# A decoder layer on one core: an opening in another order, accumulators summed two or three steps later, four tiles of the last half added on POOL

## The reference

```
x = layernorm(x + self(x))                 # 32 heads of 16, attention over the heads of one token
x = layernorm(x + cross(x, ctx_4096))      # below
x = layernorm(x + ffn(x))                  # router 64, softmax, top 8, mix of expert biases

cross: kv = concat([ctx (1601), x (256)])           # 1857 keys a batch
       q = rms_norm(x @ Wq) * qw                     # 32 heads of 128
       k = rms_norm(kv @ Wk) * kw;  v = kv @ Wv      # 8 heads of 128, 4 query heads share one
       probs = softmax(q k^T / sqrt(128));  out = (probs v) @ Wo
```

## Time and profile before

| | |
|---|---|
| median of 3 runs | 2776.49 us (2775.12 to 2777.37) |
| profiled execution | 2775.53 us, span 2773.7 us |
| PE / PEld | 2697.6 (97%) / 2188.7 (79%) |
| DVE / ACT / POOL | 2129.3 (77%) / 2097.7 (76%) / 2326.0 (84%) |
| chain of waits | PE 78%, POOL 8%, issue 7%, DVE 5%, ACT 2%, DMA 1% |

### The profile page before, as it was taken

One profiled execution on the slowest core, in us unless ns is written; L12 is line 12 of the kernel. 1 busy time (PEld: TensorE's weight loads), 2 busy tenths in 40 slices (PEclk: granted clock), 3 DMA queues, 4 the chain that ended last, 5 costly groups with the idle time before them and its releaser, 6 DMA issues.

```text
span 2773.7 us, 47580 instructions
## 1 busy us (share of the span) xinstructions
PE 2697.6 (97%) x14620; PEld 2188.7 (79%) x14620; DVE 2129.3 (77%) x3497; ACT 2097.7 (76%) x4202; POOL 2326.0 (84%) x2300
## 2 busy tenths in 40 slices
PE   7899999999999999999999999999999999999996
PEld 5777778777787888888888888888888888888763
DVE  5578777887787777777777777777777878887787
ACT  3587787787777777777788788788887877777773
POOL 4299899898888888888888888889888888888883
PEclk9999999999999999999999999999999999999998
DMA  7656655655655555555556555445544534454321
GB/s 238 241 192 216 205 200 184 219 197 178 211 175 172 180 174 179 180 183 167 171 172 203 173 183 190 158 172 169 197 157 165 189 130 163 152 167 165 121 69 42
DMA packets 160794, 485.36 MB, mean 175 GB/s; under 512 B 18583, under 2 KB 29337, under 8 KB 160542
## 3 DMA queue, kind: packets, MB, share of 16 engines
q1 hardware_dynamic: 158952, 480.75, 51.1%
q10 hardware_dynamic: 1590, 1.58, 0.2%
HBM read 402.83 MB, written 79.43 MB: 174 GB/s over the span
## 4 chain that ended last, share of the span: by engine, by line
PE 78%; POOL 8%; issue 7%; DVE 5%; ACT 2%; DMA 1%; SPq 0%; POOLq 0%; DVEq 0%; ACTq 0%
PE K_ps L1003 9%; PE K_ps L1005 9%; PE K_ps L1004 8%; PE OT_ps L1033 7%; PE S_ps L1003 7%; PE S_ps L1005 6%; PE S_ps L1004 6%; PE OT_ps L1003 5%; POOL acc L938 5%; PE OT_ps L1004 4%; PE OT_ps L1005 4%; POOL P_lo L920 2%; PE F_ps L1003 2%; PE F_ps L1004 2%; PE F_ps L1005 2%
## 5 line engine op out<-in xcount | busy, mean ns | idle before, releaser
L938 POOL TENSOR_TENSOR acc<-acc,scores 128x512 f32<-128x512 f32 x813 | 1068.6, 1314 | 50.7 <-ACT scores L1375 23.3
L920 POOL TENSOR_TENSOR P_lo<-scores,P_hi 128x512 fp32r<-128x512 f32 x672 | 901.3, 1342 | 220.8 <-ACT scores L1375 220.1
L1723 DVE SCALAR_TENSOR_TENSOR running_max<-S_ps,rk,running_max 128x512 f32<-128x512 f32 (+1 forms) x896 | 667.9, 745 | 272.9 <-ACT scores L1361 270.5
L1707 DVE TENSOR_TENSOR scores<-scores,Mb_ps 128x512 f32<-128x512 f32 (+1 forms) x960 | 645.5, 672 | 138.8 <-PE Mb_ps L1159 138.8
L1361 ACT ACTIVATE scores<-S_ps,rk 128x512 f32<-128x512 f32 (+1 forms) x960 | 652.3, 679 | 122.2 <-PE S_ps L1005 107.8
L1374 ACT ACTIVATE P_hi<-scores 128x512 fp32r<-128x512 f32 x672 | 423.4, 630 | 298.3 <-DVE scores L1707 209.5
L1375 ACT ACTIVATE scores<-scores 128x512 f32<-128x512 f32 (+1 forms) x960 | 596.7, 622 | 13.5 <-DVE scores L1707 11.9
L1003 PE MATMUL S_ps<-QT_hi,KT_hi 128*128 128x512 f32 (+1 forms) x960 | 495.5, 516 | 15.6 <-DVE running_max L1723 13.8
L1003 PE MATMUL K_ps<-Wkv_hi,kvT 128*128 128x256 f32 (+1 forms) x1664 | 470.1, 283 | 2.4 <-DVE kvT L1773 2.4
L1005 PE MATMUL K_ps<-Wkv_hi,kvT 128*128 128x256 f32 (+1 forms) x1664 | 470.3, 283 | 0.0
L1004 PE MATMUL K_ps<-Wkv_lo,kvT 128*128 128x256 f32 (+1 forms) x1664 | 469.0, 282 | 0.0
(11 more groups left out here) (244 smaller groups left out, 4577.2 us busy)
## 6 DMA issues: line engine op xcount, KB each, us to landing
kvT<-kvT_scratch SPq DMA_DIRECT2D x403, 512.0 KB, 3.9
Wq_hi<-weight_halves_scratch SPq DMA_DIRECT2D x48, 512.0 KB, 6.1
Wq_lo<-weight_halves_scratch SPq DMA_DIRECT2D x48, 512.0 KB, 6.7
Wo_hi<-weight_halves_scratch SPq DMA_DIRECT2D x48, 512.0 KB, 4.6
Wo_lo<-weight_halves_scratch SPq DMA_DIRECT2D x48, 512.0 KB, 5.7
kvT_scratch<-built SPq DMA_DIRECT2D x45, 512.0 KB, 4.2
rinv_spread<-rinv_scratch SPq DMA_DIRECT2D x63, 256.0 KB, 5.1
Wkv_hi<-weight_halves_scratch SPq DMA_DIRECT2D x24, 512.0 KB, 5.4
```

Source lines behind the costliest of these rows:

```text
L920: e.tensor_tensor(P_lo[n % PB][0:r, :], prob(t)[0:r, :], f(P_hi[n % PB][0:r, :]), ALU.subtract)\
L938: e.tensor_tensor(a[0:r, :], a[0:r, :], prob(t)[0:r, :], ALU.add).then_inc(s_acc, 1)
L1707: e.tensor_tensor(d, d, Mb_ps[0:r, :], ALU.add).then_inc(s_d, 1)
L1723: e.scalar_tensor_tensor(a, src, k, a, ALU.mult, ALU.max).then_inc(s_top, 1)
```

## The change

Three parts. First, the opening: before the first score stand KV tiles 0 to 8 (9 before), context tiles up to 11 (13), and self projections 0 to 5 (all 8); projections 5, 6, 7 go to steps -3, 3, 7. Both query tiles are normalised in one step (`normed`), QT(0, 0) goes from step -1 to -4, a Q product waits for its own half of Wq_lo only, and the self-attention's sums stand in another order. Odd context tiles of the first batch use OT_n in place of row[0] as their staging buffer. Second, for v < 32, AT of the odd half goes from c = 10 to 12 and of the even half from c = 25 to 28, with all that hangs on it. Third, in the last half tiles 0, 1, 6, 7 leave SUMMED: POOL adds them (three instructions), and DVE sums acc once.

```diff
--- before.py
+++ after.py
@@ -71,9 +71,9 @@
     TOP = 8
     FULL = [[2, 3, 6, 7, 10, 11, 14], [4, 5, 10, 11, 14], [6, 7, 14], [6, 7, 14]]
     FULL = [FULL[v // KVH] for v in range(UNITS)]
-    SUMMED = [[] for p in range(HALVES - 2)] + [[2, 4, 6, 8, 10, 12], list(range(NJ))]
+    SUMMED = [[] for p in range(HALVES - 2)] + [[2, 4, 6, 8, 10, 12], [2, 3, 4, 5, 8, 9, 10, 11, 12, 13, 14]]
     ADDED = [NJ * p + j for p in range(HALVES) for j in range(1, NJ) if j not in SUMMED[p]]
-    LATE = [p for p in range(HALVES) if len(SUMMED[p]) == NJ]
+    LATE = [HALVES - 1]
     ADD_AT = {t: n for n, t in enumerate(ADDED)}
     HALF = [[j for j in range(NJ) if j not in FULL[v]] for v in range(UNITS)]
     HALF_TILES = [NJ * p + j for p in range(HALVES) for j in HALF[p // 2]]
@@ -101,31 +101,30 @@
 
     OPENING = {
         -20: [("X", 0, 2)],
-        -19: [("X", 0, 3)],
-        -18: [("X", 0, 4)],
-        -17: [("KV", 0, 0)],
+        -18: [("X", 0, 3)],
+        -17: [("X", 0, 4), ("KV", 0, 0)],
         -16: [("KV", 0, 1)],
         -15: [("X", 0, 5)],
         -14: [("KV", 0, 2)],
         -13: [("KV", 0, 3), ("X", 0, 6)],
-        -12: [("X", 0, 7)],
-        -11: [("KV", 0, 4), ("KT", 0, 0)],
-        -9: [("X", 0, 0), ("KV", 0, 5)],
-        -8: [("Q", 0, 0, 0), ("Q", 0, 0, 1)],
-        -7: [("X", 0, 1), ("X", 0, 8)],
-        -6: [("Q", 0, 1, 0), ("Q", 0, 1, 1), ("X", 0, 9)],
-        -5: [("KV", 0, 6), ("X", 0, 10)],
-        -4: [("KV", 0, 7), ("X", 0, 11)],
-        -3: [("KV", 0, 8), ("X", 0, 12)],
-        -2: [("KV", 0, 9), ("KT", 0, 1), ("X", 0, 13)],
-        -1: [("QT", 0, 0)],
-        0: [("KV", 0, 10), ("X", 0, 14)],
-        1: [("KV", 0, 11)],
-        2: [("KV", 0, 12), ("KT", 0, 2)],
-        3: [("KV", 0, 13)],
-        4: [("KV", 0, 14)],
-        5: [("X", 1, 2)],
-        6: [("KT", 0, 3)],
+        -12: [("X", 0, 7), ("KV", 0, 4)],
+        -11: [("KT", 0, 0), ("X", 0, 0)],
+        -10: [("KV", 0, 5)],
+        -9: [("Q", 0, 0, 0), ("Q", 0, 0, 1)],
+        -8: [("X", 0, 1), ("X", 0, 8)],
+        -7: [("Q", 0, 1, 0), ("Q", 0, 1, 1)],
+        -6: [("X", 0, 9), ("KV", 0, 6)],
+        -5: [("KV", 0, 7), ("X", 0, 10)],
+        -4: [("KV", 0, 8), ("QT", 0, 0), ("X", 0, 11)],
+        -2: [("KT", 0, 1)],
+        0: [("KV", 0, 9), ("X", 0, 12)],
+        1: [("X", 0, 13), ("KV", 0, 10)],
+        2: [("KV", 0, 11)],
+        3: [("X", 0, 14), ("KT", 0, 2)],
+        4: [("KV", 0, 12)],
+        5: [("KV", 0, 13), ("X", 1, 2)],
+        6: [("KV", 0, 14)],
+        7: [("KT", 0, 3)],
         8: [("QT", 0, 1)],
         9: [("X", 1, 3)],
     }
@@ -166,7 +165,7 @@
             5: [("X", b + 1, turn(2 * h)), ("MT", 2 * v - 2)],
             7: [("Q", v, 1, 0)],
             9: [("Q", v, 1, 1)],
-            10: [("AT", 2 * v - 3)],
+            (12 if v < UNITS else 10): [("AT", 2 * v - 3)],
             11: [("O", 2 * v - 4, 0)],
             13: [("O", 2 * v - 4, 1)],
             15: [("QT", v, 0)],
@@ -175,8 +174,9 @@
             20: [("MT", 2 * v - 1)],
             21: [("O", 2 * v - 3, 0)],
             23: [("O", 2 * v - 3, 1)],
-            25: [("AT", 2 * v - 2), ("KT", v, 2)],
+            25: [("KT", v, 2)] if v < UNITS else [("AT", 2 * v - 2)],
             27: [("QT", v, 1)],
+            28: [("AT", 2 * v - 2)] if v < UNITS else [],
             29: [("X", b + 1, turn(2 * h + 1))],
         }.get(c, [])
 
@@ -204,7 +204,7 @@
 
     def splits(s):
         if s < CYCLE_0:
-            chunk = {-19: ("Wkv", 0, 0), -12: ("Wq", 0, 0), -11: ("Wq", 0, 1), 1: ("Wkv", 1, 0), 4: ("Wq", 1, 0),
+            chunk = {-19: ("Wkv", 0, 0), -11: ("Wq", 0, 0), -10: ("Wq", 0, 1), 1: ("Wkv", 1, 0), 4: ("Wq", 1, 0),
                      7: ("Wq", 1, 1)}.get(s)
         else:
             v, c = divmod(s + AHEAD, CYCLE)
@@ -220,18 +220,18 @@
 
     SELF_AT = collections.defaultdict(list)
     for t in range(SELF):
-        SELF_AT[[-20, -20, -17, -16, -15, -14, -13, -12][t]].append(("turn", t, 0))
-        SELF_AT[[-19, -18, -16, -15, -14, -13, -12, -10][t]].append(("project", t, 0))
+        SELF_AT[[-20, -20, -17, -16, -14, -13, -3, 3][t]].append(("turn", t, 0))
+        SELF_AT[[-19, -18, -16, -15, -13, -3, 3, 7][t]].append(("project", t, 0))
     SELF_AT[-18] += [("products", 0, 0)]
     SELF_AT[-17] += [("products", 1, 0), ("qk sum", 0, 0), ("qk sum", 1, 0)]
     SELF_AT[-16] += [("qk sum", 0, 1), ("qk sum", 0, 2), ("qk sum", 0, 3), ("max", 0, 0)]
-    SELF_AT[-15] += [("exp", 0, 0), ("qk sum", 1, 1), ("normalise", 0, 0)]
+    SELF_AT[-15] += [("exp", 0, 0), ("normalise", 0, 0), ("qk sum", 1, 1)]
     SELF_AT[-14] += [("qk sum", 1, 2), ("qk sum", 1, 3), ("max", 1, 0)]
-    SELF_AT[-13] += [("exp", 1, 0), ("pv sum", 0, 0), ("normalise", 1, 0)]
-    SELF_AT[-12] += [("pv sum", 0, 1), ("pv sum", 0, 2), ("pv sum", 0, 3)]
-    SELF_AT[-11] += [("residual", 0, 0)]
-    SELF_AT[-10] += [("rsqrt", 0, 0)] + [("pv sum", 1, i) for i in range(4)] + [("layernorm", 0, 0)]
-    SELF_AT[-9] += [("residual", 1, 0)]
+    SELF_AT[-13] += [("exp", 1, 0), ("normalise", 1, 0)]
+    SELF_AT[-12] += [("pv sum", 0, i) for i in range(4)] + [("residual", 0, 0)]
+    SELF_AT[-11] += [("rsqrt", 0, 0), ("layernorm", 0, 0)]
+    SELF_AT[-10] += [("pv sum", 1, 0), ("pv sum", 1, 1)]
+    SELF_AT[-9] += [("pv sum", 1, 2), ("pv sum", 1, 3), ("residual", 1, 0)]
     SELF_AT[-8] += [("rsqrt", 1, 0), ("layernorm", 1, 0)]
     EVENTS = []
     for s in range(WAIT + 4, WAIT + NS):
@@ -291,6 +291,10 @@
         return [x for at, x in ROOTED if at == s]
 
 
+    def normed(s):
+        at_once = [(v, t) for kind, v in rooted(s - 3) for t in range(TPB) if kind == "q" and v == 0]
+        return at_once + [(v, t) for t in range(TPB) for kind, v in rooted(s - 4 - t) if kind == "q" and v > 0]
+
     def pairs(s):
         return [(x[1], x[2] // 2) for x in fill(s) if x[0] == "KV" and (x[2] % 2 or x[2] == NJ - 1)]
 
@@ -325,7 +329,7 @@
     for s in STEPS:
         if 0 <= s - WAIT - 1 < NS and summed_tile(s - WAIT - 1):
             BLOCKS.append(s - WAIT - 1)
-        BLOCKS += [("acc", x[1]) for x in fill(s + 1) if x[0] == "AT" and SUMMED[x[1]] and x[1] not in LATE]
+        BLOCKS += [("acc", x[1]) for x in fill(s + 1) if x[0] == "AT" and SUMMED[x[1]]]
     BLOCK_AT = {x: n for n, x in enumerate(BLOCKS)}
 
     with ExitStack() as ctx:
@@ -586,7 +590,7 @@
             return s_ws[kind][a], 32 * (v + 1)
 
         def xrow_of(k):
-            return row[0] if k < CTX and k % 2 else xrow[:]
+            return OT_n[:] if k < CTX and k % 2 else xrow[:]
 
         def blocks_of(p):
             at = p % 2 * 256
@@ -1075,10 +1079,10 @@
                     if k >= 2:
 
                         e.wait_ge(s_kr, k - 1)
-                    if v < KVH:
-                        e.wait_ge(s_wl, W_AT["Wq", v, 1] + 1)
-                    else:
+                    if v >= KVH:
                         e.wait_ge(s_wq, 64 * (v - KVH + 1))
+                if v < KVH:
+                    e.wait_ge(s_wl, W_AT["Wq", v, part] + 1)
                 for c in range(2 * part, 2 * part + 2):
                     ins = three(K_ps[k % 2][:], xT[:, t, 0, c, :], xT[:, t, 1, c, :],
                                 Wq_hi[:, c, :], Wq_lo[:, c, :], c == 0, c == C - 1)
@@ -1534,10 +1538,8 @@
                     rsqrt(kind, v)
                 if 0 <= s < NS:
                     copy_scores(s)
-                for t in range(TPB):
-                    for kind, v in rooted(s - 4 - t):
-                        if kind == "q":
-                            normalise(v, t)
+                for v, t in normed(s):
+                    normalise(v, t)
                 for x in fill(s):
                     if x[0] in ("X", "KT", "QT"):
                         high(x)
@@ -1893,14 +1895,10 @@
                     e.tensor_reduce(sums[:, p % 2, :], added, AX.X, ALU.add, apply_transpose=True).then_inc(s_bt, 1)
                     return
                 n = len(SUMMED[p])
-                if p in LATE:
-                    e.wait_ge(s_bs, BLOCK_AT[NJ * p + NJ - 1] + 1)
-                else:
-                    e.wait_ge(s_acc, ADD_AT[NJ * p + NJ - 1] + 1)
-                    e.tensor_reduce(blocks_of(p)[:, n, :], added, AX.X, ALU.add, apply_transpose=True).then_inc(s_bs, 1)
-                    e.wait_ge(s_bs, BLOCK_AT["acc", p] + 1)
-                    n += 1
-                e.reduce_sum(sums[:, p % 2, :], blocks_of(p)[:, 0:n, :].rearrange("p k j -> p j k"), AX.X).then_inc(s_bt, 1)
+                e.wait_ge(s_acc, max(ADD_AT[t] for t in ADD_AT if t // NJ == p) + 1)
+                e.tensor_reduce(blocks_of(p)[:, n, :], added, AX.X, ALU.add, apply_transpose=True).then_inc(s_bs, 1)
+                e.wait_ge(s_bs, BLOCK_AT["acc", p] + 1)
+                e.reduce_sum(sums[:, p % 2, :], blocks_of(p)[:, 0:n + 1, :].rearrange("p k j -> p j k"), AX.X).then_inc(s_bt, 1)
 
             def divide(p):
                 e.wait_ge(s_rb, 16 * (p + 1))
```

## The result

The changed kernel takes 2782.59 us (median of 9 runs, 2780.09 to 2787.61) against 2776.49 for the kernel before (9 runs): ratio 1.0023, 95% interval 1.0015 to 1.0032. It is slower, by 6 us; I had predicted 2771.5 as likeliest and slower with .17. The time lies in the range, the sign is wrong. The profiled execution has a span of 2778.3 us, 4.6 longer than before's 2773.7.

What follows compares the result with a forecast made beforehand. PE, 97% busy, was taken to bound the kernel, leaving only its waits and the two ends; -5.5 - 7.6 - .8 + 11.5 - 2 = -4.4 from 2775.53 gave 2771.1, predicted as 2771.5, range 2758 to 2787.

Steps and rivals of the forecast that it cites:

- The opening: Before step 18: PE waits covered and half clock saved, less new idle time; -5.5 us, bounds 0 and -12.
- The two waits of 4.1: Opening: PE's waits for ACT's natq (2.44) and DVE's QT_lo (1.65) should both go, 4.1 us.
- the 2 us of new idle time: Opening: less PE work before the x1 chain and a later Wq split would together cost 2 us.
- Wq's split: Opening: POOL's split of Wq moves one step later, Q one earlier; shares the 2 us of new idle.
- the x1 chain: Opening: layernorm and xT, for which PE waits 2.84, get less PE work in front; shares the 2 us.
- The clock's -3.4: Opening: some 7 us behind the waits run at half clock; with the idle gone about 3.4 are saved.
- The odd move: Odd accumulators two steps later, divide at step 18: -7.6 from seven waits and -.8 from router units.
- the seven waits: Step 16, units 2 to 8: PE waits for the maximum behind DVE's divide meeting POOL's Wo split; -7.6, bounds -7.6 and 0.
- The router's three waits: Units with router work before step 28's maximum: three waits of .77 lose the reciprocal of .34; -.8 together.
- The even move: Step 5: PE's transposes wait for the maximum behind the divide at step 4; +11.5 us, bounds 0 and +26.
- The last half: Tail: four tiles to POOL relieve DVE, whose shifts come 2.4 earlier; -2 us, bounds +1 and -2.5.
- Rival (b): Step 4: POOL's instruction holds the even divide in most units, maximum late; up to +26, 2785.6 us; chance .15.

Runs made afterwards that it cites:

- the best kernel: Against the kernel before: repaired opening, odd move, even sum at 25, even OT_lo behind step 5's maximum except in the last unit; 2764.11 us, ratio .9956.

## Why the prediction was wrong

Its sum was -5.5 - 7.6 - .8 + 11.5 - 2 = -4.4; measured part by part it is -2.6 - 5.3 + 13.4 + 1.1 = +6.6, and the whole change measured +6.1.

- **The opening (-5.5 against -2.6).** The two waits of 4.1 were covered. The term that failed is the 2 us of new idle time: PE's idle time to step 18 did not fall by 2.1 but rose by .6, so it should have been 4.7. Wq's split, which I had named, cost 3.8, and waits for context tiles grew by 4.9, which the table shows for the tile made one step ahead and I passed over; the x1 chain, which I had also named, cost 3.3 less. The clock's -3.4 came as -3.6 in the changed kernel's execution, and in that of the opening alone, with the same tables, as +1.0. So this part of the sum is luck either way: the clock of the stretch moved by up to 4.6 us from one execution to another, more than the 2.6 measured.
- **The odd move (-8.4 against -5.3).** Six of the seven waits went, and unit 3's fell from 2.29 to .61. The step that failed is that I priced them as wholly gone. I bounded the divide at its new place by POOL's 1.3 and asked only whether DVE would be late. It was POOL that was late: I did not ask what the divide does to the five small instructions of the keys' norm that stand in front of P_lo there, and six waits of .46 to .76 came at step 19. The router's three waits, whose .8 I put here though the even sum is what leaves step 26, did not fall either: 1.07 each in the changed kernel where they were .77.
- **The even move (+11.5 against +13.4)** was right in mechanism and place: the transposes wait for the maximum behind the divide, and moving the divide behind it took 9.4 us away. That the size is near is luck. The 11.5 stood for step 5 alone, and step 5 grew by 5.1 with this move alone and by 6.6 in the changed kernel; the transposes' waits, said to reach about 15, reached 8.8. The divides there are shorter than the old ones (mean .89 alone and .99 in the whole against the 1.11 that I used; .68 in most of units 17 to 31). The rest of the loss was in places that my sum had at nothing: 3.5 at steps 7 to 9 of the router's units, where OT_lo at 6 stands in front of a shift and which I had down as free, 1.4 at step 27 and some 3 at the new place of the sum, half of it clock.
- **The last half (-2 against +1.1).** I took DVE's sums to set the pace there because DVE is busy 23.3 of 26.5 us. Taking them out altogether moved the block total by 1.1 us and the kernel's time by less than 1. Busy is not what is waited for.

So the steps that failed are the three gains: new idle time put at 2 us, removed waits priced in full, and a busy engine taken for the limit. They were to be -15.9 in all and came out as -6.8, each some 3 us short, while the one loss came out near its figure by errors that cancel. Rival (b) had the right sign with a wrong reason: the port got better, not worse. The other signs say the same: the first score was to be near 75 and came at 82.22, step 18 near 126 and came at 128.68, and the score line's wait for the maximum was to be 4 or less and is 6.0.

## What to carry to other kernels

Ask of an instruction that is moved not whether its engine has time in that step but what stands behind it in the queue and who waits for that; here one divide a unit cost 9 us in all in front of a maximum, against the same step behind it. A wait that is taken away leaves the next engine's lateness to be seen: price a removed wait only up to the next one in its place. Time each part of a change alone: two parts here won 2.6 and 5.3 us, one showed no difference, one lost 13 us, and the best kernel keeps only the first two. And when a number comes out as forecast, look whether it came from the place that was forecast: twice here it did not.

## What the runs showed of the hardware

The same instructions in the same order were granted a clock of .95 or .88 up to the first score, from one execution to another (PE busy 54.99 and 59.60 us of the same work). Inside the main loop single steps were granted .62 or .63 in some kernels and 1.00 in others, at 1.5 us a step (step 18 of unit 3, step 28 of unit 5, step 20 of unit 9). And DVE and POOL hold each other up in both directions: a POOL instruction of eight columns took .70 beside a divide of .68, its neighbours .20; a divide took 2.75 beside POOL's 2.39. Which of the two is late can hang on the start: with DVE .02 us ahead the divide took .68 and POOL 2.24, with POOL .05 ahead 2.13 and 1.63.
